# The mask of an expert layer: a matmul, or a product on VectorE with choices spread by DMA through DRAM

## The reference

```python
xf = x.reshape(-1, D)                                   # x: the layernorm of h
logits = xf @ router_w.T + router_b
idx = jnp.argmax(logits, axis=-1)                       # one of E = 32 experts for each token
h = jnp.einsum('nd,ndh->nh', xf, jnp.take(W1, idx, axis=0)) + jnp.take(b1, idx, axis=0)
h = jax.nn.relu(h)                                      # H = 16 hidden features
out = jnp.einsum('nh,nhd->nd', h, jnp.take(W2, idx, axis=0)) + jnp.take(b2, idx, axis=0)
out = jax.nn.relu(out)
```

## Time and profile before

| | us |
|---|---|
| median of 3 runs (1155.99 to 1156.19) | 1156.02 |
| the profiled execution's own time | 1155.33 |
| its span in the profile | 1153.4 |
| PE busy | 1108.9 (96%) |
| DVE busy | 490.1 (42%) |
| ACT busy | 628.5 (54%) |
| mean granted PE clock | 0.988 |

### The profile page before, as it was taken

One profiled execution on the slowest core, in us unless ns is written; L12 is line 12 of the kernel. 1 busy time (PEld: TensorE's weight loads), 2 busy tenths in 40 slices (PEclk: granted clock), 3 DMA queues, 4 the chain that ended last, 5 costly groups with the idle time before them and its releaser, 6 DMA issues.

```text
span 1153.4 us, 29598 instructions
## 1 busy us (share of the span) xinstructions
PE 1108.9 (96%) x12890; PEld 667.8 (58%) x12890; DVE 490.1 (42%) x1100; ACT 628.5 (54%) x695; POOL 10.2 (1%) x34
## 2 busy tenths in 40 slices
PE   6598999999999999999999999999999999999996
PEld 2233334345556666666666666666666666666653
DVE  6782484826345180634616263451604030311313
ACT  2354565655646565564646556564655646465552
POOL 3000000000000000000000000000000000000000
PEclk9998999999999999999999999999999999999998
DMA  5544042412104120041202121040000000000000
GB/s 149 140 111 94 4 112 65 104 39 65 38 12 111 45 68 13 11 95 39 65 11 57 40 65 39 11 94 10 11 2 11 2 10 2 11 1 6 6 2 20
DMA packets 15350, 51.68 MB, mean 45 GB/s; under 512 B 2846, under 2 KB 6046, under 8 KB 14828
## 3 DMA queue, kind: packets, MB, share of 16 engines
q1 hardware_dynamic: 15212, 49.68, 18.5%
HBM read 41.77 MB, written 4.75 MB: 40 GB/s over the span
## 4 chain that ended last, share of the span: by engine, by line
PE 91%; DVE 4%; DMA 2%; issue 1%; DVEq 1%; ACT 1%; SPq 0%; ACTq 0%
PE z_ps L623 37%; PE scores L613 36%; PE both L581 4%; PE both L596 4%; PE both L473 2%; DMA filter_ring<-filters 2%; PE both L577 1%; PE both L521 1%; PE both L511 1%; DVEq L867 1%; PE both L604 1%; DVE hres L942 1%; PE both L552 1%; PE both L561 1%; PE both L542 1%
## 5 line engine op out<-in xcount | busy, mean ns | idle before, releaser
L794 ACT ACTIVATE probs<-scores 128x1024 f32<-128x1024 f32 x480 | 465.4, 1021 | 422.0 <-PE scores L613 422.0
L613 PE MATMUL scores<-g_t,keys_t 64*64 64x512 f32 x4096 | 533.4, 594 | 4.1 <-issue 2.6
L623 PE MATMUL z_ps<-probs,keys 64*64 64x512 f32 x4096 | 532.6, 593 | 0.0
L613 PEld LDWEIGHTS scores<-g_t,keys_t 64*64 64x64 f32 x4096 | 263.8, 134 | 188.7 <-issue 71.0
L623 PEld LDWEIGHTS z_ps<-probs,keys 64*64 64x64 f32 x4096 | 248.4, 134 | 147.6 <-issue 51.7
L1019 DVE COPY o_sb<-both 128x512 f32<-128x512 f32 x14 | 9.7, 692 | 335.8 <-PE both L596 335.8
L942 DVE TENSOR_TENSOR hres<-hres,tap_product 128x504 f32<-128x504 f32 (+1 forms) x128 | 89.1, 696 | 10.5
L937 DVE SCALAR_TENSOR_TENSOR tap_product<-filter_ring,w,xin 128x504 f32<-128x504 f32 (+1 forms) x120 | 89.0, 742 | 5.6 <-DMA filter_ring<-filters 2.1
L581 PE MATMUL both<-y_t,w 64*64 64x512 f32 x464 | 68.2, 597 | 0.0
L787 ACT ACTIVATE hidden<-both 128x1024 f32<-128x1024 f32 (+1 forms) x58 | 58.5, 1009 | 3.0 <-PE both L581 3.0
L1086 DVE COPY z_sb<-z_ps 128x512 f32<-128x512 f32 x16 | 11.1, 692 | 113.2 <-PE z_ps L623 113.2
(11 more groups left out here) (130 smaller groups left out, 588.6 us busy)
## 6 DMA issues: line engine op xcount, KB each, us to landing
filter_ring<-filters SPq DMA_DIRECT2D x90, 384.0 KB, 5.2
out_dram<-out_sb SPq DMA_DIRECT2D x32, 128.0 KB, 2.4
xin<-x_dram SPq DMA_DIRECT2D x6, 528.0 KB, 8.2
g_t<-g_t SPq DMA_DIRECT2D x24, 128.0 KB, 4.8
hidden<-once_dram SPq DMA_DIRECT2D x1, 930.0 KB, 13.1
hidden<-once_dram SPq DMA_DIRECT2D x1, 576.0 KB, 4.8
filters<-filters_sb SPq DMA_DIRECT2D x30, 18.0 KB
xin<-x_dram SPq DMA_DIRECT2D x1, 384.0 KB, 6.1
```

Of the source, the lines that this page charges most:

```text
L613: last = T.matmul(scores[rows_of(h), c, r * 512:(r + 1) * 512], keys_t[rows_of(r), n // NQ % 2, g * 128 + 64 * h:g * 128 + 64 * h + 64], g ...
L623: last = T.matmul(z_ps[rows_of(c), h, :], keys[rows_of(h), n // NQ % 2, 2 * g + r, :], probs[rows_of(h), (2 * g + c) % RING, r * 512:(r + ...
L794: A.activation(probs[:, unit % RING, :], scores[:, c, :], ACT.Exp, scale=SCALE if n else first_scale[:, 0:1]).then_inc(probs_ready, 1)
```

## The change

Twelve of the sixteen blocks (`CHOSEN_BY_DMA`, m = 2 to 13) no longer use the mask matmuls. SP stores `onehot_t` to DRAM (two DMAs of 32 rows of 1 KB), waits until that has landed, and reads it back with four DMAs, each of which writes every expert's choice to the 16 rows of its hidden features (`chosen`, 128 rows of 2 KB each). DVE then computes max(PSUM, 0) times `chosen` in one instruction, where ACT had computed Relu. So that DVE and the DMAs come in time, the order of the fills changes in the blocks from 3 on: the layernorm behind `sum2` becomes a fill of its own (`ln`, group 7, behind `lg`), `ot` moves from group 10 to 8, `xt` and `g` from 8 and 9 to 9 and 10, `hid0` to `hid3` from 11 to 14 to 12 to 15, `o2` from 15 to 16. On SP, the new DMAs stand between the second and the third part of the filters.

```diff
+CHOSEN_BY_DMA = range(2, BLOCKS - 2)
 def usual_groups(n):
-    groups = merged({1: at(m - 1, "fin"), 2: at(m, "pz"), 4: at(i, "sum2"), 5: at(m, "yt"), 6: at(m, "lg")}, pair,
-                    {8: at(i, "xt"), 9: at(i, "g"), 10: [*at(m, "ot"), *at(j, "sum0 sum1")]})
-    if n < BLOCKS - 1:
-        return merged(groups, {11: at(m, "hid0"), 12: at(m, "hid1"), 13: at(m, "hid2"), 14: at(m, "hid3"),
-                               15: at(m, "o2")})
+    groups = merged({1: at(m - 1, "fin"), 2: at(m, "pz"), 4: at(i, "sum2"), 5: at(m, "yt"), 6: at(m, "lg"),
+                     7: at(i, "ln")}, pair, {8: at(m, "ot"), 9: at(i, "xt"), 10: [*at(i, "g"), *at(j, "sum0 sum1")]})
+    if m in CHOSEN_BY_DMA:
+        return merged(groups, {12: at(m, "hid0"), 13: at(m, "hid1"), 14: at(m, "hid2"), 15: at(m, "hid3"), 16: at(m, "o2")})
...
+    choices = nc.dram_tensor("choices", (BLOCKS, E, 2, 512), BF16).ap()
+        chosen = sb("chosen", [128, FT, 2, 512], BF16)
...
+            def spread_choices(i):
+                ot = f"ot@{i}"
+                sp.wait_ge(drained[places.of[ot]], places.nth[ot])
+                for c in range(2):
+                    sp.dma_start(choices[i, :, c, :], onehot_t[64 * c:64 * c + E, :]).then_inc(choices_stored, 16)
+                sp.wait_ge(choices_stored, 32 * (i - CHOSEN_BY_DMA[0] + 1))
+                for f in range(FT):
+                    rows = choices[i, f * 128 // H:(f + 1) * 128 // H, :, :].rearrange("e c n -> e (c n)")
+                    sp.dma_start(chosen[:, f, :, :].rearrange("p c n -> p (c n)"),
+                                 rows.unsqueeze(1).broadcast_to([128 // H, H, 2 * 512])
+                                 ).then_inc(choices_loaded, 16)
...
-                    spread_filters(n + NQ + 1)
+                    spread_filters(n + NQ + 1, range(CHUNKS - 1))
+                if n - 1 in CHOSEN_BY_DMA:
+                    spread_choices(n - 1)
+                if n > 1 and n + NQ + 1 < BLOCKS:
+                    spread_filters(n + NQ + 1, range(CHUNKS - 1, CHUNKS))
...                                   # PE, hid: the mask only where i not in CHOSEN_BY_DMA
-                                            start=False, stop=True)
+                                            start=i in CHOSEN_BY_DMA, stop=True)
...                                   # DVE
-                    if part == CHUNKS - 1:
-                        layernorm(i)
+                if name == "ln":
+                    layernorm(i)
+                    return
+                if name.startswith("hid") and i in CHOSEN_BY_DMA:
+                    f, k = int(name[3:]), places.of[full]
+                    dve.wait_ge(choices_loaded, 16 * FT * (i - CHOSEN_BY_DMA[0] + 1))
+                    dve.wait_ge(filled[k], places.nth[full])
+                    V.scalar_tensor_tensor(hidden[:, f, :, :], place[k][:, :, :], 0.0, chosen[:, f, :, :], ALU.max,
+                                           ALU.mult).then_inc(drained[k], 1)
+                    return
```

More of the change, by code:

```diff
@@ L59 @@
 KEPT_AT, KEPT_N = columns(KEPT)
-NONE = ("sum", "pow", "aw")
+NONE = ("sum", "ln", "pow", "aw")
+CHOSEN_BY_DMA = range(2, BLOCKS - 2)
 USUAL, FIRST_TAP, TAP_PLACES = 0, 1, 6
@@ L86, in opening_groups @@
              *at(0, "pow3 pow4 pow5"), *at(3, "cv"), *at(0, "xt g")],
-        0: at(1, "sum0 sum1 sum2"),
+        0: at(1, "sum0 sum1 sum2 ln"),
         3: at(1, "xt"),
-        4: [*at(1, "g"), *at(2, "sum0 sum1 sum2")],
+        4: [*at(1, "g"), *at(2, "sum0 sum1 sum2 ln")],
         7: at(2, "xt"),
-        8: [*at(2, "g"), *at(3, "sum0 sum1 sum2")],
+        8: [*at(2, "g"), *at(3, "sum0 sum1 sum2 ln")],
         11: at(3, "xt"),
@@ L104, in early_groups @@
     m, i, j = n - 1, 2 * n + 2, 2 * n + 3
-    usual = {2: at(m, "pz"), 3: at(i, "sum0 sum1"), 5: at(m, "yt"), 6: at(m, "lg"), 7: at(i, "sum2"), 8: at(m, "ot"),
+    usual = {2: at(m, "pz"), 3: at(i, "sum0 sum1"), 5: at(m, "yt"), 6: at(m, "lg"), 7: at(i, "sum2 ln"), 8: at(m, "ot"),
              9: at(m, "hid0"), 10: at(m, "hid1"), 11: at(i, "xt"), 12: at(i, "g"), 13: at(m, "hid2"),
@@ L108, in early_groups @@
     if n == 1:
-        return merged(usual, {3: at(j, "cv"), 12: at(j, "sum0 sum1 sum2"), 16: at(j, "xt")})
+        return merged(usual, {3: at(j, "cv"), 12: at(j, "sum0 sum1 sum2 ln"), 16: at(j, "xt")})
     return merged({0: at(i - 1, "g"), 1: at(m - 1, "fin")}, usual,
@@ L263, in vit_block_kernel @@
         lower_copied = sem("lower_copied")
+        choices_stored, choices_loaded = sem("choices_stored"), sem("choices_loaded")
         y_ready, onehot_ready = sem("y_ready"), sem("onehot_ready")
@@ L326, in store_filters, with spread_filters @@
                                      ).then_inc(filters_stored, 16)
-            def spread_filters(i):
+            def spread_choices(i):
[9 more added lines that the diff above has]
+                                 ).then_inc(choices_loaded, 16)
+            def spread_filters(i, parts=range(CHUNKS)):
                 sp.wait_ge(filters_stored, filters_stored_with(i))
-                for part in range(CHUNKS):
+                for part in parts:
                     slot, before = slot_of(i, part)
@@ L576, in fill @@
                         for c in range(2):
-                            T.matmul(mine[rows_of(c), r, :], mask_w[rows_of(r), cols[c]], onehot_t[rows_of(r), :],
-                                     start=True, stop=False)
+                            if i not in CHOSEN_BY_DMA:
+                                T.matmul(mine[rows_of(c), r, :], mask_w[rows_of(r), cols[c]], onehot_t[rows_of(r), :],
+                                         start=True, stop=False)
                     for r in range(2):
```

## The result

| | before | after |
|---|---|---|
| median of the runs, us | 1156.01 (1155.63 to 1156.19) | 1166.63 (1162.77 to 1176.48) |
| ratio to before, 95% interval | | 1.0108 [1.0075, 1.0142] |
| the profiled execution, us (span) | 1155.33 (1153.4) | 1164.88 (1162.9) |

What follows compares the result with a forecast made beforehand. PE's own instructions were taken to bound the attention blocks. Mask -10.3, o2 stall +0.6, xt stall +0.75 and load waits +13.5 gave +4.6 us: 1160.6 us forecast for the median, range 1146 to 1168.

Steps and rivals of the forecast that it cites:

- What bounds the kernel: In the attention blocks only PE's own instructions set the time; PE was busy for 96% of the span.
- the mask: Leaving out the mask matmuls saves PE 0.214 us in each of 48 hid fills, 10.3 us off.
- The product on DVE: DVE's 1024-column product takes 1.24 us (1.1 to 1.5), hidden between hid fills but not before o2.
- The stall before o2: PE waits about 0.05 us for hid3's product in each of 12 blocks, 0.6 us on (0 to 3.6).
- the 0.15 us from a DVE result to PE: Assumed delay between the end of a DVE result and the start of the PE work waiting for it.
- The order on DVE: keys comes late for xt in group 9: 0.15 us stall in five odd blocks, 0.75 us on (0 to 1.5).
- Place and cause of the waits: PE waits before hid1 in blocks 4, 6, 8, 10, because the loads run on eight engines and land late.
- the 13.5 of the sum: Waits before hid1: 3.55 us in three even blocks, 2.85 in block 10; 13.5 us on (0 to 20).
- T: Time for the 1.05 MB of the four loads, 9.9 us (5.0 to 11.5); PE loses T - 6.35 us.
- the forecast's 1.1 and 0.6 us: Allowances around the loads: 1.1 us from issue until data moves, 0.6 us after the last byte.
- The rate: Each of the loads' eight engines runs at the slow 14.1 GB/s, not the fast 26.1.
- every wait put in lengthens it in full: Any wait put into PE's work in the attention blocks lengthens the kernel by that wait's full length.

Runs made afterwards that it cites:

- e1_const: Changed kernel without storing or loading the choices; the product reads a constant 1: 1145.10 us, 0.9909 of the kernel before.
- e8_stall3: e1_const with four idle VectorE instructions ahead of hid0's product in blocks 4, 6, 8, 10, giving 3.35 us waits: 1163.17 us, ratio 1.0074.
- e4_sixteen: Changed kernel with hidden rows reordered so the loads' source has 16, not 8, as outermost dimension: 1148.34 us, 0.9944 of the kernel before.
- e9_stall6: e1_const with six idle VectorE instructions ahead of hid0's product in blocks 4, 6, 8, 10, giving 5.96 us waits: 1174.62 us, ratio 1.0166.
- e6_act_store: Changed kernel with ScalarE instead of SyncE issuing the two stores of the choices, right behind its copy: 1149.66 us, 0.9950 of the kernel before.
- e11_again: The changed kernel run once more, unedited, on another occasion; source of its second profile: 1166.09 us, 1.0095 of the kernel before.

## Why the prediction was wrong

- **What bounds the kernel; the mask.** Right: the full window of the earlier trace rows carries the first. 0.217 us a fill, against 0.214 from the earlier trace rows; in e1_const the time from DVE's first copy of `z_ps` to its last is 982.2 us, 10.1 less than before.
- **The product on DVE.** Right in size (1.225 us each, 1.24 from the earlier trace rows). The stall before o2 did not come: PE starts it 1.72 us after the weighing (452.72 to 454.44 in block 5). 0 instead of 0.6. The product for hid3 ended at 454.29, in time; and the 0.15 us from a DVE result to PE, taken from another fill in the earlier trace rows, were too many: before hid1 PE starts 0.06 us after the product (516.04 to 516.10).
- **The order on DVE.** Right: in block 5, xt starts at 427.77, 0.11 us later than its turn, 0.15 forecast.
- **Place and cause of the waits.** Right: only blocks 4, 6, 8, 10, only before hid1, loads on eight engines (eight small packets each, a DMA share of 0.50) as the packet counts of the earlier trace rows had suggested.
- **Length of the waits.** 13.9 us in the first profile for the 13.5 of the sum, but this closeness is partly luck. The blocks had 1.4, 5.7, 4.6 and 2.1 us where the sum had 3.55 in three and 2.85 in the last. The stores were done 0.6 to 1.6 us later than worked out from the earlier trace rows, measured against the group they stand in; T, with the forecast's 1.1 and 0.6 us taken off the times above, was 7.2, 10.6, 10.0 and 8.7 us, 9.1 on average for 9.9, and the two misses nearly cancel. In the second profile T was 10.1 on average and the waits 17.3 us. The rate was not the one I chose, either. From 503.5 to 508 the DMAs moved 162 GB/s at a share of 0.45, as of eight engines alone: some 20 GB/s each and not 14. After that the share is about 1, with the third filter part and the query copies issued behind the loads:

```profile
503.50:508.00 4.50, 4.50 (x48) 2.57 (x44) 2.17 (x4) 2.50 (x3) 0.00 (x0) 1.00 0.45 162
508.00:511.00 3.00, 2.67 (x26) 1.03 (x18) 0.00 (x0) 1.15 (x2) 0.00 (x0) 1.00 1.09 221
```

- **The step that failed: a wait was priced at its own length.** The first reading of the trace said that "every wait put in lengthens it in full", and the sum stopped there. A wait of some us also costs the clock behind it: 3.6 us in the first profile, 8.0 in the second, up to 3.0 behind one wait of 3.35 in e8_stall3. The trace of before showed it, in the opening, and I did not use it: after a wait of 4.65 us in front of xt, the weighing took from 97.54 to 100.96, 3.42 us instead of 1.72.

```profile
96.66 1.13 PE L473 MATMUL both<-w,keys 64*64 64x64 f32 x32 [4.65 <-DVE keys L901]
97.54 3.66 PE L623 MATMUL z_ps<-probs,keys 64*64 64x512 f32 x16
100.96 2.65 PE L613 MATMUL scores<-g_t,keys_t 64*64 64x512 f32 x16
```

  The granted clock was 0.50 there (98 to 100 us). In the first profile the attention blocks come to +7.7 us with this cost and to +4.1 without it; in the second to +15.4 and +7.4, since the waits were longer too. The median of +10.6 lies between the two. Of the first profile's +9.6, 2.5 us more lie outside the attention blocks, and no run ties them to the change.
- **The spread.** Not forecast at all. The changed kernel spread over 14 us on the first chip and 11 on the second, where the kernel before spread over 0.6 and 4.9. The versions in which no hid fill waits spread over 1.8 to 5.9 us. e4_sixteen, whose loads land close to the limit, spread over 12.

What stays open: why the stores take 6.5 to 8.8 us beside filters even from another queue, how much of the loads' time is the third filter part's, and why the clock fell behind two of four equal waits.

## What to carry to other kernels

Where TensorE is full, an edit that takes matmuls out is worth the distance between the starts (0.217 us a fill here), and it is worth it only if every new result comes before its turn. Price a wait with the slower clock that may come behind it, not at its length: here it came behind most waits of 2.9 to 6.0 us and cost up to 3.0 us. When several DMAs feed several steps, give each its own semaphore: the first step then waits for a quarter of the bytes, which here turned 1.1% slower into 0.9% faster with no transfer sped up. Before a DMA goes on a tight path, look at the outermost dimension of its source: with 8 the four loads here took 8.9 to 12.3 us from the first issue to the product, with 16 6.7 to 8.1.

## What the runs showed of the hardware

- A DMA from SP whose source had 8 as its outermost dimension and whose destination had 128 rows ran on eight engines: 8 small packets for each of 48 loads (3614 = 2846 + 384 + 384) and a DMA share of 0.50 while the loads moved alone (429.5 to 432.0 us); with 16 it ran on sixteen (3998, and 0.91 from 428.0 to 430.0 us of e4_sixteen).
- 1024 float32 columns from PSUM times a bfloat16 tile took 1.225 us on VectorE, as 256 and 512 float32 columns extrapolate (1.24 us). The idle instruction of e9_stall6, 1024 columns from PSUM without a bfloat16 operand, took 1.224 us, so that operand gained nothing.
- Two stores of 32 KB took 1.9 us (425.65 to 427.59) with nothing else moving. Behind filter loads of 384 KB each, four of them in the even blocks, they took 7.5 to 8.5 us from SyncE's queue in the changed kernel, and 6.5 to 7.6 us from ScalarE's in e6_act_store.
- In attention blocks where TensorE otherwise never waited, its granted clock stayed at 1.00 behind waits of 1.4 and 2.1 us (first profile of the change). It fell to 0.50 behind one of 2.9 us (e11_again, block 10), behind two of four waits of 3.35 us (e8_stall3) and behind all nine of 4.1 to 6.0 us (the change, e11_again, e9_stall6). Where it fell, 1.4 to 3.0 us were lost.
